# Scores of windowed attention as three products by row parity, with transfers through DRAM in fewer pieces

## The reference, cut to what matters

```
xn   = batch norm of x;  q, k, v = conv1x1(xn), 6 heads of 16 channels, 4 images
attn = conv7x7(concat(q * 16**-0.5, k)) + dm_b + rel_bias        # 32 channels -> 49 scores
attn = softmax(attn over the 49)
out  = sum over the 7x7 window of v's patches * attn             # 16 channels
x1   = x + conv1x1(out);  result = x1 + c2(gelu(c1(x1)))
```

## Time and profile before

| what | value |
|---|---|
| median of 3 runs | 1270.98 us (1269.72 to 1272.98) |
| the profiled execution's own time | 1271.44 us |
| its span, first to last instruction | 1269.3 us |
| mean granted TensorE clock | 0.923 of full speed |
| busy share of PE, DVE, ACT, POOL | 85%, 78%, 43%, 69% |
| attention layer within the span | from about 786 us to the end |

### The profile page before, as it was taken

The page is one execution under the profiler, slowest core; times in us unless marked ns, Lnnn a source line. Parts: engine busy times, 40 slices in busy tenths (PEclk is TensorE's granted clock), DMA queues, the critical chain, the costliest instruction groups (busy, mean ns, idle before and its releaser), DMA issues. The chain is left out here.

```text
span 1269.3 us, 9544 instructions
## 1 busy us (share of the span) xinstructions
PE 1083.1 (85%) x3294; PEld 371.7 (29%) x3294; DVE 985.5 (78%) x695; ACT 545.8 (43%) x572; POOL 881.8 (69%) x349
## 2 busy tenths in 40 slices
PE   7789999799989989989878695899999699990567
PEld 2233333233323323323322231233333233330122
DVE  1399999899998999989999997000969695967683
ACT  5755866796747557566656240120120201010212
POOL 0079899897978697879897765000779794979770
PEclk8779999899999999989999998699999899995678
DMA  3144355434354435543544531846495649526002
GB/s 75 68 136 149 147 154 133 151 131 149 129 153 119 150 116 149 159 142 117 166 134 132 165 133 30 158 79 109 102 169 114 124 77 192 89 45 119 21 1 70
DMA packets 107639, 150.95 MB, mean 119 GB/s; under 512 B 75450, under 2 KB 76192, under 8 KB 106824
## 3 DMA queue, kind: packets, MB, share of 16 engines
q1 hardware_dynamic: 105992, 145.01, 44.2%
q10 hardware_dynamic: 1600, 5.34, 1.4%
HBM read 123.27 MB, written 10.70 MB: 106 GB/s over the span
## 5 line engine op out<-in xcount | busy, mean ns | idle before, releaser
L690 POOL TENSOR_TENSOR hc<-h,c_rep 128x1024 f32<-128x1024 f32 x192 | 451.3, 2359 | 178.2 <-DVE h L734 170.4
L734 DVE TENSOR_TENSOR_SCAN h<-a,bu 128x1024 f32<-128x1024 f32 x192 | 439.0, 2287 | 22.2 <-ACT a L564 4.6
L390 PE MATMUL y_ps<-hc,ident 128*128 128x512 f32 x768 | 381.5, 620 | 2.9 <-POOL hc L690 1.7
L564 ACT ACTIVATE a<-dt,a_neg 128x1024 f32<-128x1024 f32 x192 | 218.3, 1146 | 224.0 <-DVE h L734 218.5
L724 DVE TENSOR_TENSOR bu<-bu,u 128x1024 f32<-128x1024 f32 x192 | 232.1, 1209 | 16.9 <-PE bu L369 16.9
L1145 POOL TENSOR_TENSOR prod_p<-vw,at 128x3584 f32<-128x3584 f32 x18 | 130.8, 7264 | 153.8 <-DMA vw<-v_d 128.4
L390 PEld LDWEIGHTS y_ps<-hc,ident 128*128 128x128 f32 x768 | 144.0, 196 | 210.1 <-issue 187.4
L1028 PE MATMUL sc_ps<-x,w_up 128*64 128x512 f32 x672 | 179.7, 609 | 2.5 <-DMA x<-qk 2.5
L1028 PE MATMUL sc_ps<-x,w_low 96*64 96x512 f32 x672 | 178.1, 604 | 0.0
L369 PE MATMUL bu<-st,pick 96*64 96x512 bf16 (+1 forms) x512 | 118.5, 390 | 49.2 <-DVE h L734 45.1
L1166 DVE TENSOR_TENSOR acc_ps<-acc_ps,prod_v 128x512 f32<-128x512 f32 x156 | 109.1, 699 | 5.4
(11 more groups left out here) (122 smaller groups left out, 942.8 us busy)
## 6 DMA issues: line engine op xcount, KB each, us to landing
c_rep<-c_d SPq DMA_DIRECT2D x128, 512.0 KB, 3.7
c_rep<-c_d SPq DMA_DIRECT2D x128, 256.0 KB, 3.9
vw<-v_d SPq DMA_DIRECT2D x24, 532.0 KB, 9.2
x<-qk SPq DMA_DIRECT2D x72, 171.0 KB, 3.8
scores_d<-sc ACTq DMA_DIRECT2D x24, 196.0 KB
at<-scores_d SPq DMA_DIRECT2D x24, 196.0 KB, 5.1
x<-qk SPq DMA_DIRECT2D x24, 152.0 KB, 3.9
v_d<-v SPq DMA_DIRECT2D x24, 76.0 KB, 5.2
```

The source lines that it names most:

```text
L390: mm = pe.matmul(y_ps[:, cols(th)], ident[:, :], hc[:, k % HC_RING, cols(th)], start=(n == 0 and d == 0), stop=(n == N_ST - 1))
L564: nc.scalar.activation(a[:, k % A_RING, :], dt[:, tile % 2, :], ACT.Exp, scale=a_neg[:, kind_of(tile), n:n + 1]).then_inc(exp_done, 1)
L690: nc.gpsimd.tensor_tensor(hc[:, k % HC_RING, :], h[:, k % H_RING, :], c_rep[:, k % C_RING, :], ALU.mult).then_inc(hc_done, 1)
L734: nc.vector.tensor_tensor_scan(scan_order(h[:, k % H_RING, :], d), scan_order(a[:, k % A_RING, :], d), scan_order(bu[:, k % 2, :], d), 0.0 ...
```

## The change

**Scores.** With even and odd rows apart, the result at even rows and at odd rows is made from three half-size products, on the odd rows of the padded input with `w_both = w_even + w_odd`, on the difference even minus odd with `w_even`, and on the difference of the next even row minus odd with `w_odd`. The first product is evacuated to `sc[:, :, 2]` and added to each of the other two by a matmul with the identity. A pair takes 3 x 7 steps and 2 steps of the identity. Tensors are in parity order from there on.

**Differences.** `qk` now has four planes, odd rows, even rows and two differences; DVE makes the differences, two subtractions of 128 (or 64) partitions by 722 and 684 elements for each of two head groups of each batch image: before the first tile for batch images 0 and 1, behind window row 0 of tiles 0 and 1 for batch images 2 and 3.

**Transfers.** Planes are stored to DRAM (`qk_d`) and loaded into `x4` from there, three loads an image, each of up to 128 runs of 2432 B; for pairs 2 to 11 ACT issues them, six after its stores of pair p for pair p + 2. v is stored in one transfer a batch image, and `vw` is loaded in eight transfers a tile, in runs of 1064 B. The output goes in one transfer a batch image.

**Order.** `qkv` of batch images 1, 2, 3 stands behind pairs 0, 1, 2. The exponentials on ACT stand behind the places of `EXP_AFTER` (pair, evacuation). `maximum(j + 1)` stands on DVE ahead of the last window row of tile j. The MLP of batch image 0 is spread behind pairs 8, 9, 10 on PE. `DVE_MLP` has new places; among them the projection of batch image 1 ahead of window row 1 of tile 4. `load_o` of batch image b follows `store_o` and `load_tile` in the steps `LOAD_O`. Six of eight statistics are made at the end of `mamba`. DVE's adds take two slices at a time into a PSUM tile of two slices.

The core of the diff:

```diff
-DVE_MLP = {(4, 7): ((0, 0),), (5, 0): ((0, 8),), (5, 1): ((1, 0),), (5, 2): ((1, 8),), (5, 3): ((2, 0),), (5, 7): ((2, 8),)}
+DVE_MLP = {(3, 0): ((0, 0),), (4, 0): ((0, 8),), (4, 1): ((1, 0),), (4, 3): ((1, 8),), (5, 2): ((2, 0),),
+           (5, WIN): ((2, 8),)}
+MLP0_AFTER = {8: (0, 1), 9: range(2, 8), 10: (8, 9)}
+GELU0_AFTER = 9
+EXP_AFTER = ((1, 2), (3, 2), (6, 0), (8, 1), (10, 2))
+LOAD_O = (1, 3, 4, 5)
+DIFFERENCES = ((0, 0), (1, 0))
...
+            for n in range(2 * B - 2):
+                left(dve, J("out", 4, n // 2, 1) if n // 2 == 2 else J("out", 4, 3, 1))
+                nc.vector.bn_stats(bn_stats[:, n, :], x1[:, n // 2, cols(n % 2)])
             gate(5)
...
+        def load_odd(eng, image):
+            b, hd = divmod(image, HEADS)
+            p, slot = image // 2, image % X4_RING
+            eng.wait_ge(odd_stored[hd // 4], 16 * (b + 1))
+            src = qk_d[image, 0, 0]
+            eng.dma_start(x4[:, slot, 0, :, :].rearrange("p y x -> p (y x)"),
+                          bass.AP(src.tensor, src.offset, [[HP, 4], [3 * HH * HP, 2 * HD], [1, H // 2 * HP]]))\
+                .then_inc(odd_in[p % 2], 16)
+        def load_dif(eng, image):
+            b, hd = divmod(image, HEADS)
+            p, slot = image // 2, image % X4_RING
+            eng.wait_ge(dif_stored[hd // 4], 16 * (b + 1))
+            for plane, taps in ((1, 4), (2, 3)):
...
             def load_tile(j):
...
                 for i in range(4):
-                    src = v_d[4 * j + i]
-                    win = bass.AP(src.tensor, src.offset, [[V_ROW, H], [1, WIN * V_ROW]])
+                    for e in range(2):
+                        src = v_d[4 * j + i, 0]
+                        win = bass.AP(src.tensor, src.offset + e * HP,
+                                      [[2 * HP, H // 2], [HP * HP, HD], [1, WIN * HP]])
...
+            for b in range(1, B):
+                for m in range(2):
+                    store_odd(b, m)
+                    store_dif(b, m)
+                store_v(b)
+                if b < 3:
+                    load_tile(b - 1)
+            for j in range(TILES):
                 store_o(j)
-                load_o(LAST_TILE.index(j))
+                if j + 2 < TILES:
+                    load_tile(j + 2)
+                if j in LOAD_O:
+                    load_o(LOAD_O.index(j))
...
             def score(p):
+                both, even, odd = 3 * p, 3 * p + 1, 3 * p + 2
+                for n, w, rows, plane in ((both, w_both, 128, 0), (even, w_even, 128, 1), (odd, w_odd, 96, 2)):
...
+                    if n >= 2:
+                        pe.wait_ge(sc_out, n - 1)
                     for dx in range(WIN):
+                        for i in range(2):
+                            mm = pe.matmul(sc_ps[64 * i:64 * i + 64, n % 2, :], w[0:rows, dx, :],
+                                           x4[0:rows, (2 * p + i) % X4_RING, plane, :, dx:dx + W],
+                                           start=(dx == 0), stop=(n == both and dx == WIN - 1))
+                    if n != both:
+                        pe.wait_ge(sc_out, both + 1)
+                        mm = pe.matmul(sc_ps[:, n % 2, :], eye[:, :], sc[:, p % 2, 2, :], start=False, stop=True)
                     mm.then_inc(scored, 1)
...
                 if m < 2:
+                    if b and th == 0:
+                        act.wait_ge(odd_stored[m], 16 * b)
+                        act.wait_ge(differed, 2 * (2 * b - 2 + m) + 2)
...
             for p in range(PAIRS):
                 store_scores(p)
+                if p + 2 < PAIRS:
+                    load_x4(p + 2)
+                if p + 1 < B:
                     for i in range(6):
+                        qkv(p + 1, i)
+                if (p, 2) in EXP_AFTER:
+                    exps(EXP_AFTER.index((p, 2)))
+                if p == GELU0_AFTER:
+                    mlp(0)
+            for b in range(1, B):
+                if b == 2:
+                    exps(TILES - 1)
                 mlp(b)
...
+            def row(j, dy):
...
+                if dy == 0:
+                    product(nc.vector, j, dy, 0, 2, e, acc_v).then_inc(pv, 1)
+                    product(nc.vector, j, dy, 2, WIN, e, prod_v[:, 2:]).then_inc(pv, 1)
...
+                for k in range(2 * n - 2, WIN - 1, 2):
+                    dve.wait_ge(pv, base + n)
+                    nc.vector.tensor_tensor(acc_v, acc_v, prod_v[:, k:k + 2], ALU.add).then_inc(pv, 1)
...
                 for dy in range(DVE_ROWS[j]):
+                    if dy == DVE_ROWS[j] - 1 and j + 1 < TILES:
+                        maximum(j + 1)
                     for m, i in DVE_MLP.get((j, dy), ()):
                         mlp_out(m, i)
                         mlp_out(m, i + 1)
+                    row(j, dy)
+                    if (j, dy) in DIFFERENCES:
+                        for m in range(2):
+                            differences(2 + DIFFERENCES.index((j, dy)), m)
```

More of the change, by code:

```diff
@@ L30 @@
 HP = H + 2 * R
-V_ROW = HD * HP
 IMAGES = B * HEADS
@@ L906, in _ @@
                 second += [(rel[rows, :], t["rel_bias"][:, i::2]), (dm_b[rows, :], t["dm_b"])]
[L907 to L934, removed]
+            third = [(proj_w[:, :], t["proj_w"]), (proj_b[:, :], t["proj_b"]), (c1_w[:, :], t["c1_w"]),
+                     (c1_b[:, :], t["c1_b"]), (c2_w[:, :, :], t["c2_w"]), (c2_b[:, :], t["c2_b"])]
@@ new lines, in _, with store_odd, store_dif @@
+            assert [len(first), len(second), len(third)] == L1_LOADS
+            def store_odd(b, m):
+                heads = (4, 2)[m]
+                left(sp, ("qkv", b, 2 * m + 1))
+                sp.dma_start(qk_d[HEADS * b + 4 * m:HEADS * b + 4 * m + heads, :, 0].rearrange("i c n -> (i c) n"),
+                             qk[0:32 * heads, m, 0, :, :].rearrange("p y x -> p (y x)"))\
+                    .then_inc(odd_stored[m], 16)
+            def store_dif(b, m):
+                heads = (4, 2)[m]
+                sp.wait_ge(differed, 2 * (2 * b + m) + 2)
+                sp.dma_start(qk_d[HEADS * b + 4 * m:HEADS * b + 4 * m + heads, :, 1:].rearrange("i c s n -> (i c) s n"),
+                             qk[0:32 * heads, m, 2:4, :, :].rearrange("p s y x -> p s (y x)"))\
+                    .then_inc(dif_stored[m], 16)
@@ L989, in _ @@
-            load_o(1)
-            for j in range(TILES - 2, TILES):
+            with nc.allow_non_contiguous_dma(reason="small weights"):
+                for dst, src in first:
+                    sp.dma_start(dst, src).then_inc(loaded[0], 16)
+                sp.wait_ge(padded, 1)
+                for dst, src in second:
+                    sp.dma_start(dst, src).then_inc(loaded[1], 16)
+            sp.wait_ge(zeroed, 1)
+            store_odd(0, 0)
+            load_odd(sp, 0)
+            load_odd(sp, 1)
@@ new lines, in _ @@
+            store_dif(0, 0)
+            load_dif(sp, 0)
+            load_dif(sp, 1)
+            for image in (2, 3):
+                load_odd(sp, image)
+            for image in (2, 3):
+                load_dif(sp, image)
+            store_odd(0, 1)
+            store_dif(0, 1)
+            store_v(0)
+            with nc.allow_non_contiguous_dma(reason="small weights"):
+                for dst, src in third:
+                    sp.dma_start(dst, src).then_inc(loaded[2], 16)
+            for b in range(1, B):
[5 more added lines that the diff above has]
+                    load_tile(b - 1)
@@ L991, in _ @@
+            for j in range(TILES):
                 store_o(j)
-                load_o(LAST_TILE.index(j))
+                if j + 2 < TILES:
+                    load_tile(j + 2)
+                if j in LOAD_O:
+                    load_o(LOAD_O.index(j))
             for b in range(B):
[L994 to L997, removed]
+                left(sp, ("mlp", b, 9))
+                sp.dma_start(t["out"][b], x1[:, b, :]).then_inc(out_s, 16)
@@ L1008, in bank, with bias @@
                 return g_ps[:, job % G_BANKS, :]
+            def bias(m):
+                n = JOB["bias", m]
+                free(n)
+                w = (slice(0, 128), slice(128, 192), slice(192, 288))[m]
+                pe.matmul(bank(n)[0:w.stop - w.start, 0:1], qkv_w[:, w], bn_shift[:, :], start=True,
+                          stop=True).then_inc(job_done, 1)
             def qkv(b, i):
@@ L1055, in _ @@
             pe.wait_ge(bn_step, BN_DONE)
[L1056 to L1060, removed]
-            for i in range(6):
-                qkv(0, i)
+            for m in range(3):
+                bias(m)
+                for i in range(2):
+                    qkv(0, 2 * m + i)
             pe.wait_ge(loaded[1], 16 * L1_LOADS[1])
+            pe.wait_ge(w_ready, 1)
             for p in range(PAIRS):
                 score(p)
-                if p % 3 == 0 and p // 3 + 1 < B:
+                if p + 1 < B:
                     for i in range(6):
-                        qkv(p // 3 + 1, i)
-            for b in range(B):
```

(25 more changed lines are left out.)

307 lines of the change are left out of this document (161 added, 146 removed).

## The result

| | before | changed |
|---|---|---|
| median of the runs | 1270.35 us | 1425.89 us (1423.89 to 1427.25, 4 runs) |
| ratio, with 95% interval | | 1.122 (1.120 to 1.125) |
| profiled execution, its span | 1271.44, 1269.3 us | 1423.89, 1422.0 us |

The forecast was 1281 with a range up to 1299. The sign was right; 143.4 us of span (1422.0 against 1278.6) had no place in the sum. The state-space layer ends no later than before (its last add begins at 780.1 us of the span, in the kernel before at 784.9), so all of it is in the attention layer.

A forecast was written before the change was run, and what follows sets the result against it. Scores (49 us a tile) and products (47 plus 7) were taken as nearly balanced; a chain of waits gave T5 = 1203, then last tile 49.1, tail 23.0, output 2.5 + 1 and 2.1 around the span: 1281 us, range 1257 to 1299.

The forecast's parts named there:

- With 128 long rows each I take 0.6, so 3.6 (ends: 2.5 and 7.0): ScalarE's queue after a pair: six plane loads issue in 0.6 us each, 3.6 in all, between 2.5 and 7.0.
- Short value runs: Value loads before a tile: runs of 1064 B instead of 17 KB cost nothing; if not, tile starts waiting for values move.
- The qkv after a pair: The next image's q, k, v, after ScalarE's plane-load issues, take TensorE 4.75 us.
- P0: End of the first pair's scores on TensorE: 808 + 20.2 + 2.8 = 831 us.
- P1: End of the second pair's scores on TensorE: 831 + 5 + 4.75 + 20.2 = 861 us.
- P2: End of the third pair's scores on TensorE: 891 us.
- The step that decides: VectorE in tile 4: image 1's projection add stands ahead of row 1, holding VectorE from near 1130 to 1169.5 us; T5 = 1203.
- o's landing: Load of o, queued behind a tile's value loads: lands in 12.9 us, 25.4 after P11.
- o of image 1 can't come before P11: Argument against the rival that GpSimd sets the pace (1209 us, chance 0.05): this o is queued behind tile 5's loads.
- the subtractions: VectorE's differences of images 2 and 3 inside tiles 0 and 1: 10.4 and 14.3 us, bounds 3.6 to 18.
- T5 to the end: After tile 5's start: last tile 49.1 us, tail 23.0, output 3.5, together 75.6.
- The rival of transfers that land sooner: Both loads of o land 9.4 us sooner each, giving 1262 us, or 1249 with free subtractions; chance 0.25.

The follow-up runs named there:

- spread: Changed kernel with plane loads ordered channels outermost (32), taps inside, and a zero-weight fourth tap for the difference plane; 1336.30 us, 1.052 of the kernel before.
- both: Changed kernel with plane loads ordered 32 channels outermost and the values' old layout of 17 KB runs put back; 1319.90 us, 1.039 of the kernel before.
- o first: Against both: the load of o issued ahead of the next tile's loads, for every batch image; 1271.80 us, 1.001 of the kernel before.
- split: Changed kernel with each plane load cut into one load per tap, same bytes to the same places, no zero tap; 1362.64 us, 1.073 of the kernel before.

## Why the prediction was wrong

Starts of tiles on GpSimd (T0 to T5), end of the last pair's scores (P11) and length of the span, forecast and measured, in us of the span:

| | T0 | T1 | T2 | T3 | T4 | P11 | T5 | span |
|---|---|---|---|---|---|---|---|---|
| forecast | 885.5 | 958 | 1015 | 1064 | 1118 | 1139.5 | 1203 | 1278.6 |
| changed | 933.2 | 1030.5 | 1107.6 | 1178.1 | 1254.6 | 1274.7 | 1346.1 | 1422.0 |
| spread | 895.6 | 976.6 | 1043.5 | 1097.4 | 1163.9 | 1185.6 | 1257.1 | 1333.0 |
| both | 893.5 | 972.7 | 1037.9 | 1087.0 | 1153.9 | 1175.6 | 1242.9 | 1317.5 |
| o first | 896.7 | 973.4 | 1038.9 | 1088.0 | 1138.7 | 1160.4 | 1196.3 | 1271.5 |

**The step that failed** is "With 128 long rows each I take 0.6, so 3.6 (ends: 2.5 and 7.0)". It counted rows and length and not how many engines a pattern reaches. Measured: 11 to 12 us after the first pairs (16.33 for four loads after a later one), and, what the forecast had no term for, the score loads' 21 us of issue instead of 3.8, five times over. The upper end of 7 came from SyncE's copies, each with 32 partitions outermost on both sides, so the range was blind on that side too. Spread shows its price, 89.0 us of span (1422.0 to 1333.0) of the 143.4; split shows that the cause is the engines reached.

**Short value runs "costed at nothing"** was wrong too: 16.4 us once isolated. The text named it as what would move every tile start; the range did not include it. But the runs are the smaller part of the values' delay. From the first value load's issue to the tile's start, where values are the last to come, the kernel before takes 14.4 to 14.9 us (four loads of 32 partitions), both takes 19.2 to 20.4 (17 KB runs too, but eight loads of 16 partitions), spread 20.5 to 23.7 (1064 B runs). And the low rate is not that of short runs alone: 127 GB/s at a share of 1.09 with them, 126 at 0.94 with 17 KB runs (both, 956 to 972). The forecast gave the eight loads 0.6 for their issue and nothing more. No run goes back to four loads a tile, so that they cost the 5 us is argued, not shown.

**The qkv after a pair**, "4.75", was mis-sized, by some 5 us behind pairs 0 and 1. This remains when transfers are mended. TensorE's timeline in the o-first kernel:

```profile
863.01 1.88 PE L1067 MATMUL g_ps<-x,qkv_s 96*128 96x512 f32 x4
...
870.61 7.33 PE L1067 MATMUL g_ps<-x,qkv_s 96*64 96x512 f32 x8 [5.72 <-ACT qk L1152]
```

It fills two banks, waits 5.7 us for ScalarE, which is issuing plane loads, and then runs eight at half pace (the granted clock between 862 and 880 is 0.66): 14.9 us in place of 9.75 with its wait. In both, P0 came at 824.7, 6 before the forecast's 831, and P1 at 861.3. That P1 agrees with the forecast's 861 is luck: an early start and a longer gap (36.6 for 30) cancel. P2 came at 898.5 instead of 891.

**The step that decides** held as a mechanism. The changed kernel's VectorE waits where the forecast put it, and SyncE issues o behind tile 5's loads (1279.87 and 1283.27 are their issues):

```profile
1288.49 0.65 SPq L992 DMA_DIRECT2D o<-o_d  x1
...
1310.33 0.75 DVE L1299 SCALAR_TENSOR_TENSOR x<-g_ps,proj_b,x 96x512 f32<-96x512 f32 x1 [45.72 <-PE g_ps L1087]
```

A wait of 30 to 40 was forecast, 45.7 came; from P11 to T5 63.5 was forecast, 71.4 came. The size of o's landing was off: 12.9 taken, 19.7 measured at both places that matter. And the forecast's "o of image 1 can't come before P11" is true of the queue's order alone: o first undid it, which is 31.4 of its 46.6 us.

**Right:** a pair with nothing late took 20.8 us (20.2); the subtractions 10.0 us in tile 0 (10.4); 1.232 us for an add of 1024 elements (1.21); 3.88 for a product (3.9); T5 to the end 75.9 (75.6). The subtractions in tile 1 took 10.1 in the changed kernel and 15.9 in both, on either side of the 14.3 taken. The rival of transfers that land sooner was wrong altogether, and a page's rule stood for it. By the Trainium skill (DMA: Bandwidth & Descriptors, Anatomy of one DMA) one o of 384 KB would land in an estimated 2.9 us (2.0 plus bytes at 436 GB/s). The page gives this fit for transfers that GpSimd issues; these are SyncE's. The rows show 3.5 when o is first and 19.67 behind other loads.

The near agreement of the forecast (1281) with o first (1271.8) is no merit: in o first the terms that were too small and the wait for o that the experiment took out cancel.

What stays open is most of the 39 us between the forecast and both (1317.5 against 1278.6). The table gives the places: 8 by T0, 15 by T1, 23 by T2, 36 by T4, of which 13 between T3 and T4, where image 0's o is waited for. The first 8 can be read: T0 comes 32.2 us after P1 where 24.3 was taken, with the score loads issued 0.8 later and taking 2.9 more to issue, and the value loads 4.1 more. No run divides the others.

## What to carry to other kernels

For every transfer that a change adds, look at the outermost dimension of source and destination before its bytes: with 4 or 3 steps there these loads got a quarter of the transfer engines (share 0.24), and they also held up the queue that issued them and broad loads on another queue. Fewer transfers are not cheaper transfers: 22 loads over all engines beat 6 over four by 63 us. When two engines are nearly balanced, a saving on one pays only as far as the other, the transfers and the order of each queue let it through; here the small edit on VectorE alone gave at least as much as the whole change in any form that was run, and the loads of o moved ahead in a queue were worth 48 us.

## What the runs showed of the hardware

A queue that is behind shows up in the duration of its issue rows: four score loads took 21.0 us to issue on SyncE while ScalarE's narrow loads were in flight, 8.15 with these spread, 3.35 with none. Busy transfer engines need not move much: a share of 1.09 carried 127 GB/s (values in 1064 B runs), 0.94 carried 126 (in 17 KB runs, 16 partitions a load), and 0.99 carried 333 (spread planes and stores). And one small load's time is set by its place: 384 KB landed in 3.5 us ahead of a tile's loads and in 19.67 behind them.
